# Where the identity of a graph convolution is added: on the vector engine in the third pass too, instead of by products with an identity matrix

## What is computed

```python
h = relu(layernorm(x)); x = x + (adj/rowsum(adj)) @ h @ W_in + (adj.T/colsum(adj)) @ h @ W_out
h = relu(layernorm(x)); x1 = silu(adj @ h @ W + b); x = x + silu(adj @ x1 @ W + b)
h = relu(layernorm(x)); x = x + relu((D @ (adj + I) @ D) @ h @ W + b)
h = relu(layernorm(x)); x = x + relu((D @ (adj + I) @ D) @ (h @ W) + b)
# D = diag(rsqrt(rowsum(adj + I)))
```

## Time and profile before

| | us |
|---|---|
| median of 3 runs (lowest, highest) | 1126.58 (1125.49, 1129.52) |
| the profiled execution's own time | 1127.55 |
| span in its profile | 1125.8 |
| PE, PEld busy | 1106.7, 914.0 |
| DVE busy | 1047.5 |
| ACT busy | 912.6 |
| POOL busy | 48.0 |

### The profile page before, as it was taken

The page is one execution under the profiler, slowest core; times in us unless marked ns, Lnnn a source line. Parts: engine busy times, 40 slices in busy tenths (PEclk is TensorE's granted clock), DMA queues, the critical chain, the costliest instruction groups (busy, mean ns, idle before and its releaser), DMA issues.

```text
span 1125.8 us, 14740 instructions
## 1 busy us (share of the span) xinstructions
PE 1106.7 (98%) x5056; PEld 914.0 (81%) x5056; DVE 1047.5 (93%) x1452; ACT 912.6 (81%) x1278; POOL 48.0 (4%) x40
## 2 busy tenths in 40 slices
PE   6999999999999999999999999999999999999998
PEld 4778888888888888888888888888888888788886
DVE  6899997999999999989988999999999999998987
ACT  6999987798888688888887888888778778877774
POOL 0000000000000000000000211111111111100000
PEclk9999999999999999999999999999999999999999
DMA  9999998999999899999999999999999999999992
GB/s 327 402 383 404 404 409 318 344 383 409 376 368 348 300 409 409 409 400 363 342 367 377 348 363 356 357 373 333 400 341 354 364 367 326 338 410 374 383 362 114
DMA packets 113835, 408.36 MB, mean 363 GB/s; under 512 B 12640, under 2 KB 13920, under 8 KB 113760
## 3 DMA queue, kind: packets, MB, share of 16 engines
q1 hardware_dynamic: 113760, 407.42, 95.5%
HBM read 405.27 MB, written 2.10 MB: 362 GB/s over the span
## 4 chain that ended last, share of the span: by engine, by line
PE 79%; DVE 13%; DMA 3%; ACT 2%; issue 2%; SPq 1%; ACTq 0%; DVEq 0%
PE bank L737 50%; PE bank L741 25%; DVE a_lo L516 9%; PE bank L758 3%; DMA raw<-in_adj_t_dram 3%; ACT a_hi L381 1%; DVE stats L547 1%; ACT a_hi L383 1%; DVE h_lo L516 1%; SPq L323 1%; DVE x_sb L611 1%; PE bank L799 0%; SPq L332 0%; DVE h_lo L540 0%; DVE acc L604 0%
## 5 line engine op out<-in xcount | busy, mean ns | idle before, releaser
L516 DVE TENSOR_TENSOR a_lo<-raw,a_hi 128x1024 fp32r<-128x1024 f32 x560 | 658.5, 1218 | 39.1 <-ACT a_hi L381 22.1
L737 PE MATMUL bank<-a_hi,h_hi 128*128 128x512 f32 x1400 | 437.5, 394 | 10.9 <-DVE h_lo L540 10.2
L741 PE MATMUL bank<-a_lo,h_hi 128*128 128x512 f32 x1400 | 434.3, 391 | 2.4 <-DVE a_lo L516 1.7
L381 ACT ACTIVATE a_hi<-raw 128x1024 fp32r<-128x1024 f32 x368 | 376.4, 1055 | 71.4 <-PE bank L741 54.3
L737 PE MATMUL bank<-a_hi,h_lo 128*128 128x512 f32 x1400 | 432.4, 390 | 0.0
L741 PEld LDWEIGHTS bank<-a_lo,h_hi 128*128 128x128 f32 x1400 | 261.7, 188 | 64.4 <-DVE a_lo L516 10.8
L737 PEld LDWEIGHTS bank<-a_hi,h_hi 128*128 128x128 f32 x1400 | 259.1, 188 | 64.1 <-DVE h_lo L540 10.2
L737 PEld LDWEIGHTS bank<-a_hi,h_lo 128*128 128x128 f32 x1400 | 263.4, 188 | 55.6
L383 ACT ACTIVATE a_hi<-raw 128x1024 fp32r<-128x1024 f32 x192 | 201.8, 1054 | 27.2 <-PE bank L741 12.2
L516 DVE TENSOR_TENSOR a_lo<-acc,a_hi 128x1024 fp32r<-128x1024 f32 x144 | 169.9, 1219 | 10.6 <-ACT a_hi L381 9.2
L381 ACT ACTIVATE a_hi<-acc 128x1024 fp32r<-128x1024 f32 x144 | 148.7, 1055 | 28.6 <-PE bank L741 26.9
(11 more groups left out here) (75 smaller groups left out, 420.9 us busy)
## 6 DMA issues: line engine op xcount, KB each, us to landing
raw<-in_adj_t_dram SPq DMA_DIRECT2D x496, 512.0 KB, 6.9
acc<-in_adj_t_dram SPq DMA_DIRECT2D x144, 512.0 KB, 6.7
raw<-in_adj_dram SPq DMA_DIRECT2D x128, 512.0 KB, 7.0
out_dram<-x_sb SPq DMA_DIRECT2D x7, 256.0 KB, 6.8
x_sb<-in_x_dram SPq DMA_DIRECT2D x3, 512.0 KB, 11.7
x_sb<-in_x_dram SPq DMA_DIRECT2D x2, 256.0 KB, 4.0
out_dram<-x_sb SPq DMA_DIRECT2D x2, 128.0 KB, 1.7
w_sb<-in_L_gnn_W_dram SPq DMA_DIRECT2D x3, 64.0 KB, 10.3
```

The costliest lines, as they stand in the source:

```text
L381: act.activation(sub_hi_of(n), sub_raw(n), ACT.Copy).then_inc(sub_hi, 1)
L516: dve.tensor_tensor(sub_lo_of(n), sub_raw(n), sub_hi_of(n).bitcast(F32), ALU.subtract).then_inc(sub_lo, 1)
L737: pe.matmul(bank[half][:, :], weights, hi_a[:, half * GW:(half + 1) * GW], start=start and weights is hi_w, stop=False)
L741: last = pe.matmul(bank[half][:, :], hi_w, lo_a[:, half * GW:(half + 1) * GW], start=False, stop=stop)
```

## The change

The identity is added by DVE in pass 3 as in pass 4: `plus_cols` now holds 64 substeps, those of both passes. `PLUS_AHEAD` goes from 2 to 5 for both. `identity_product`, its call, `AT_OWN`, the tile `ident_r` with ACT's copy into it, and PE's wait for that copy are gone.

```diff
-        ident_r = sb("ident_r", [P, P], F32R)
...
-        PLUS_AHEAD = 2
+        PLUS_AHEAD = 5
         plus_cols = {}
         plus_n = {}
-        for g in range(NG):
-            for b in range(CB):
-                n = n_of(SWEEPS, g, g * CB + b)
-                plus_n[n] = len(plus_cols)
-                plus_cols[n] = slice(b * P, (b + 1) * P)
+        for sweep in (3, 4):
+            for g in range(NG):
+                for b in range(CB):
+                    n = n_of(sweep, g, g * CB + b)
+                    plus_n[n] = len(plus_cols)
+                    plus_cols[n] = slice(b * P, (b + 1) * P)
...
-        AT_OWN = 20
...
-                if n == 40:
-                    act.wait_ge(ident_made, 2)
-                    act.activation(ident_r[:, :], ident[:, :], ACT.Copy).then_inc(ident_made, 1)
...
-            def identity_product(sweep, g, bank):
-                src = SET_OF[sweep - 1]
-                for half in range(2):
-                    for b in range(GB):
-                        for part in (h_hi[src], h_lo[src]):
-                            pe.matmul(bank[half][:, b * P:(b + 1) * P], part[:, CB * g + GB * half + b, :], ident_r[:, :],
-                                      start=False, stop=False, skip_group_check=True)
...
-            pe.wait_ge(ident_made, 3)
...
-                        if sweep == 3 and s == AT_OWN:
-                            identity_product(sweep, g, bank)
```

## The result

The changed kernel takes 1132.38 us (median; 1131.80 to 1134.16), against 1126.57 (1125.49 to 1129.52) for the kernel before, timed beside it: a ratio of 1.0052 with an interval of 1.0042 to 1.0062. Repeated later on another occasion it was 1131.77 against 1126.40, 1.0046 (1.0033 to 1.0059). So it is slower by about 0.5%, 5.4 to 5.8 us. The forecast was +3.6, to 1130.2; the median lies in its outer range (1127 to 1134.5) and 0.4 above the narrower one of its favoured rival A (1128.6 to 1132). The profiled execution took 1132.48 us with a span of 1130.7, 4.9 longer than before.

A forecast was written before the change was run, and what follows sets the result against it. In pass 3 DVE and PE were taken as level, with DVE becoming the bound. The sum 6.5 - 1.2 - 0.4 - 0.8 - 0.3 - 0.2 = +3.6 us took the median from 1126.58 to 1130.2, range 1127 to 1134.5.

The forecast's parts named there:

- rival A: DVE takes over as the bound, in part hidden: +3.6 us, from +2 to +5.4; chance 0.65.
- The point on which all hung: In pass 3 DVE needs 47.03 us a group and PE 47.18; PE may get faster by 0.15 only.
- Additions on DVE, those in the loops free: Pass 3's 32 additions: +6.5 us; those in DVE's waits for ACT after layer norm free: -1.2, pass 4's group 0 -0.4.
- The waits of 0.45 and 0.46: DVE's idle time falls to 0.45 us from 1.06 at s = 14 of group 2 and s = 30 of pass 3's last group.
- The mark forecast near 896: DVE's output step at substep 5 in pass 3, at 893.24 before, moves near 896; that of 941.70 near 945.5.
- DVE's waits for PE, -1.1 in all: Pass 3: the 0.83 us wait ahead of 798.88 goes, -0.8; two groups of 47.18 instead of 47.03 give -0.3.
- The products bring nothing more: Deleting pass 3's identity products saves PE 7.0 us of work, but brings nothing beyond the 1.1 already counted.
- From the last wait on PE is the bound again: From 971.84 in pass 4 PE is never short of a split: DVE needs 41.5 us a group against 45.33.
- The copy at line 454, -0.2: ACT's rounded identity held its queue 0.29 us, 0.2 net of overlap; removing it gives between 0 and -0.2, taken as -0.2.
- The wait for the tile five ahead, 0: In DVE's queue: eight splits, at least 9.1 us, cover loads that land after 8.5 at the latest, so 0.
- rival C: Additions stall DVE waiting for the tile five substeps on, from group 1 of pass 3: +4 on A, 1134.2; chance 0.17.
- Rival D: All 6.5 us land on DVE; loops stretch and waits for PE stay: +6.5 - 0.2, 1132.9; chance 0.10.

## Why the prediction was right, and where it was short

The point on which all hung, DVE at 47.03 us a group against PE at 47.18, was right: with no identity in pass 3 DVE's marks are 47.04 us apart. The size was short: +3.6 was forecast and +5.4 to +5.8 measured, at or beyond the end of A's own range (+5.4). By the steps of the sum:

- **Additions on DVE, those in the loops free.** Right. DVE's marks moved as the steps say: from 799.64 to 847.68 and to 895.71 are 48.04 and 48.03 us, forecast 47.03 + 5 x 0.204 = 48.05 each. The waits of 0.45 and 0.46 stand where they were named. The mark forecast near 896 is at 895.71; the next, forecast near 945.5, is at 946.62 and holds DVE's wait for POOL.
- **DVE's waits for PE, -1.1 in all.** Right: 1.17 by the kernel without the products. The wait ahead of 798.88 is gone; the mark moved by 0.76 there, while the additions alone would give five and three times 0.204, 1.6.
- **The products bring nothing more.** Right: 0.2 us beside the additions.
- **From the last wait on PE is the bound again.** Right: groups of 45.33, and the last wait and the end are late by the same 4.9.
- **The copy at line 454, -0.2.** No run shows it. The copy is at 73.2 us, and the first weight product of pass 2 varies by 3.2 us between executions, so 0.2 can't be found there; with the unused copy put back nothing fell out of the scatter.
- **The wait for the tile five ahead, 0.** Right in every profile: DVE never waited for a load in passes 3 and 4, so rival C's mechanism did not happen. Its heading, that the additions stall DVE, did come true, by another way (below). ACT did wait once for an addition, 0.60 us at 921.96; the prediction had ruled that out.

Without the copy the sum is +3.8 us for the span; the two profiles with all additions on DVE, no products, no long root and no more in the loops give +3.66 (562.43 less 558.77) and +3.62 (562.39). **What was short is the list of things that an addition can touch.** The prediction asked what waits in the queues of DVE, ACT and SP and does not mention POOL; it put at nothing, without a reason, what an addition can do to POOL's 2.95 us of `std` and `rstd`. With an addition right behind the statistics `std` can be held up until DVE runs dry: in the changed kernel `std` ended at 930.92, and DVE had stopped for want of work at 930.87, behind three splits and three additions. The norm loop then comes 1.2 us late, in the pass in which DVE sets the pace. With one such event +3.7 becomes +4.9, which is the profile; with two it would be +6.1 (an estimate; no profile has two). The median of +5.4 to +5.8 lies between the two, and it was +3.5 with the four additions moved. But it was also +3.6 in the run with additions and products, where both places stand as they were, and +3.9 with only one addition moved. How often the roots are long in an execution that isn't profiled was not seen. So the wait of 1.2 us in a profile is shown, and that the rest of the median's surplus over +3.7 comes from such waits is likely and not shown.

The Trainium skill (SBUF — State Buffer, SBUF: two separate sides) says that of a DVE instruction with two inputs in SBUF and a GpSimd instruction that reads SBUF, whichever starts first holds the other off for the whole of its instruction. The traces agree as to the pair: `std` always ends 0.05 or 0.06 us after a split, `rstd` is 1.01 us when DVE stands still and 1.86 beside splits, and some splits grow when POOL adds. The four long cases go beyond it: the 3.96 us are three splits and not one. This rule spoke against the change, and weighing it would have pointed at POOL; the prediction looked at occupancy instead.

Rival D, the whole 6.5 us on DVE, came closest by its number, 1132.9, and that is luck: the loops did take their additions and the waits for PE did go.

## What to carry to other kernels

Where two engines take the same time for a stretch, taking work off one is worth only the difference, here 1.2 of 7.0 us, and giving it to the other costs most of it, here 4.8 of 6.5 us (562.39 with the additions less 557.62 without any identity); the page's busy shares don't show this, the distance between equal marks on each engine's timeline does. Work moved to the engine that sets the pace belongs into the waits that it has anyway: five additions in a loop of 3.5 us cost nothing, while five between splits cost 1.0 (5 x 0.204), and moving ten of them into loops brought 1.8 us (562.39 to 560.63). And when an instruction is put between others, look also at what another engine is doing at that moment, not only at who waits for whom.

## What was not expected of the hardware

- An addition of 4 elements a partition on POOL took 3.76 to 3.96 us instead of 1.09 in 4 of the 11 cases in which a two-input addition of 128 columns on DVE had put the split behind it on the same start, to 0.02 us. It took 1.29 in the other seven with the same neighbours. What decides between the two stays open.
- The same small addition ended 0.05 or 0.06 us after the end of a 1024-column subtraction on DVE in all 208 records.
- POOL's power of 4 elements took 1.01 us with DVE idle, 1.86 beside DVE's splits and 2.07 beside a split and an addition.
- The 59 additions on POOL from 700 to 1100 us took 0.45 to 5.4 us each, for the same 128 x 128 elements.
- The first 566 us vary by 3.2 us from execution to execution; in two profiles of the kernel before, the 559 behind them agree within 0.1.
